# One exponential over both heads' scores in an attention and feed-forward kernel

## The reference

```python
x = x + xattn(layernorm(x), ctx, mask, g_norm, null_kv, Wq, Wkv, Wout, g_out)
x = x + ffn(layernorm(x), k0, k1, k2, s0, s1, s2)
```

## Time and profile before

| | us |
|---|---|
| median of three runs | 1582.44 |
| span of the profiled execution | 1574.0 |
| time around the span (median less span) | 8.4 |
| TensorE matmul busy | 1513.6 |
| VectorE busy | 1032.6 |
| GpSimd busy | 777.9 |
| ScalarE busy | 708.4 |
| of that the exponentials of line 777, 832 of them | 527.5 |
| attention steps, first to last score matmul | 130.3 to 1326.3 |

### The profile page before, as it was taken

One profiled execution on the slowest core, in us unless ns is written; L12 is line 12 of the kernel. 1 busy time (PEld: TensorE's weight loads), 2 busy tenths in 40 slices (PEclk: granted clock), 3 DMA queues, 4 the chain that ended last, 5 costly groups with the idle time before them and its releaser, 6 DMA issues.

```text
span 1574.0 us, 20245 instructions
## 1 busy us (share of the span) xinstructions
PE 1513.6 (96%) x6068; PEld 845.3 (54%) x6068; DVE 1032.6 (66%) x1272; ACT 708.4 (45%) x1169; POOL 777.9 (49%) x657
## 2 busy tenths in 40 slices
PE   5898999999999999999999999999999998999998
PEld 3554555455545544554455445554554453778777
DVE  7784677577767766776677567757776747544442
ACT  3324444644464446445544554455445534232242
POOL 3005666576656665666566566656665646101100
PEclk9998999999999999999999999999999999999999
DMA  5222100110020002000200020003000501101000
GB/s 160 79 82 68 51 7 7 34 57 8 12 60 26 7 16 77 7 8 14 77 7 8 15 77 7 11 10 84 8 8 21 178 7 61 61 14 53 13 14 14
DMA packets 43586, 60.22 MB, mean 38 GB/s; under 512 B 4049, under 2 KB 31636, under 8 KB 42580
## 3 DMA queue, kind: packets, MB, share of 16 engines
q1 hardware_dynamic: 43476, 58.92, 12.7%
HBM read 26.27 MB, written 17.30 MB: 28 GB/s over the span
## 4 chain that ended last, share of the span: by engine, by line
PE 89%; DVE 5%; issue 2%; ACT 2%; POOL 1%; DMA 0%; DVEq 0%; SPq 0%; ACTq 0%; POOLq 0%
PE ps_o L1244 25%; PE ps_s L1263 17%; PE ps_s L1264 12%; PE ps_side L1182 12%; PE ps_side L1325 10%; PE ps_side L1168 3%; PE ps_s L1286 3%; PE ps_side L1203 2%; PE ps_side L1158 1%; PE ps_side L1159 1%; DVE mxh L925 1%; PE ps_side L1191 1%; PE ps_o L1142 1%; PE ps_o L1144 1%; DVE khl L914 1%
## 5 line engine op out<-in xcount | busy, mean ns | idle before, releaser
L424 POOL TENSOR_TENSOR acc<-acc,prob 128x512 f32<-128x512 f32 x522 | 669.1, 1299 | 338.5 <-ACT prob L777 311.9
L777 ACT ACTIVATE prob<-ps_s,keybias 128x512 f32<-128x512 f32 x832 | 527.5, 685 | 560.7 <-PE ps_s L1264 518.4
L925 DVE TENSOR_REDUCE mxh<-ps_side 128x1 f32<-128x804 f32 x512 | 485.6, 991 | 152.9 <-PE ps_side L1182 150.3
L1244 PE MATMUL ps_o<-prob,vp 128*64 128x512 f32 x1664 | 448.2, 616 | 0.0
L1263 PE MATMUL ps_s<-qdup,khl 128*128 128x512 f32 x832 | 373.0, 448 | 9.2 <-issue 4.6
L1263 PEld LDWEIGHTS ps_s<-qdup,khl 128*128 128x128 f32 x832 | 156.1, 188 | 365.5 <-issue 261.9
L1264 PE MATMUL ps_s<-qrest,krest 128*128 128x512 f32 x832 | 329.5, 396 | 0.0
L1182 PE MATMUL ps_side<-khl,qdup 128*128 128x402 f32 x1024 | 249.3, 360 | 10.5 <-ACTq L716 4.2
L1182 PEld LDWEIGHTS ps_side<-khl,qdup 128*128 128x128 f32 x1024 | 187.3, 189 | 58.5 <-DVE mxh L925 22.3
L424 DVE TENSOR_TENSOR acc<-acc,prob 128x512 f32<-128x512 f32 x182 | 166.8, 918 | 60.5 <-ACT prob L777 50.2
L1264 PEld LDWEIGHTS ps_s<-qrest,krest 128*128 128x128 f32 x832 | 157.3, 189 | 19.0 <-issue 0.4
(11 more groups left out here) (130 smaller groups left out, 1039.3 us busy)
## 6 DMA issues: line engine op xcount, KB each, us to landing
o_scratch<-onorm SPq DMA_DIRECT2D x32, 256.0 KB, 2.1
otb<-o_scratch SPq DMA_DIRECT2D x4, 2048.0 KB, 8.1
qdup<-qdup SPq DMA_DIRECT2D x14, 512.0 KB, 5.3
v_scratch<-vsb SPq DMA_DIRECT2D x13, 512.0 KB, 3.2
krest<-khl SPq DMA_DIRECT2D x16, 416.0 KB, 5.1
vp<-v_scratch SPq DMA_DIRECT2D x8, 832.0 KB, 7.4
xs<-in_x SPq DMA_DIRECT2D x4, 512.0 KB, 6.8
xres<-in_x SPq DMA_DIRECT2D x1, 2048.0 KB, 11.1
```

Of the source, the lines that this page charges most:

```text
L424: eng.tensor_tensor(a, so_far, prob[g][s % RING][:, :], ALU.add).then_inc(sum_done[g], 1)
L777: act.activation(prob[g][s % RING][:, :], ps_s[g][:, :], ACT.Exp, bias=keybias[:, kt:kt + 1], scale=SCALE).then_inc(p_made[g], 1)
L925: dve.reduce_max(mxh[:, g, qt, half:half + 1], ps_side[slot][:, :, 0:MXW], AX.XY).then_inc(side_free[slot], 1)
L1244: last = pe.matmul(ps_o[qb % 2][hi_rows(g), :], vp[u][:, kt, hi_rows(g)], prob[g][s % RING][:, :], start=(kt == 0), stop=(kt == KT - 1))
```

## The change

The two PSUM tiles of the scores become one tile of two banks, and `ps_s[g]` are its halves. The two rings `prob[g]` become one ring whose tiles hold both heads, and `prob[g][r]` are their halves. ScalarE waits for both heads' scores and both heads' sums and for `pv_done`, and then issues one exponential over 2 x 512 columns. The two semaphores `p_made[g]` become one, which this exponential raises by one. All waits for `p_made[g]` (in `add_tile`, in `values` and ahead of each head's scores) become waits for it. The matmuls, the sums, the side jobs and their order are the same.

```diff
--- before.py
+++ after.py
@@ -256,7 +256,8 @@
         cT1 = sb("cT1", [C1, KPAD])
         at["vp0"] = at[""]
         vp = [sb(f"vp{u}", [P, KT, P]) for u in range(2)]
-        prob = [[sb(f"prob{g}{r}", [P, QW]) for r in range(RING)] for g in range(2)]
+        prob_both = [sb(f"prob{r}", [P, 2, QW]) for r in range(RING)]
+        prob = [[prob_both[r][:, g, :] for r in range(RING)] for g in range(2)]
         acc = [[sb(f"acc{g}{r}", [P, QW]) for r in range(2)] for g in range(2)]
         x_lo = sb("x_lo", [P, DC, SEQ], F32R)
         onorm = sb("onorm", [P, QW])
@@ -318,7 +319,8 @@
         assert at["small"] <= end_operands0, (at["small"], end_operands0)
 
 
-        ps_s = [psum(f"ps_s{g}", [P, 512]) for g in range(2)]
+        ps_both = psum("ps_s", [P, 2, 512])
+        ps_s = [ps_both[:, g, :] for g in range(2)]
         ps_o = [psum(f"ps_o{r}", [P, 512]) for r in range(2)]
         ps_side = [psum(f"ps_side{r}", [P, 2, 512]) for r in range(2)]
         ps_c = ps_s
@@ -353,7 +355,7 @@
         mx_made, row_made = sem("mx_made"), [sem("row_made0"), sem("row_made1")]
         s_made = [sem(f"s_made{g}") for g in range(2)]
 
-        p_made = [sem(f"p_made{g}") for g in range(2)]
+        p_made = sem("p_made")
         pv_done = sem("pv_done")
         sum_done = [sem(f"sum_done{g}") for g in range(2)]
         o_copied = sem("o_copied")
@@ -418,7 +420,7 @@
 
             qb, kt = s // KT, s % KT
             a = acc[g][qb % 2][:, :]
-            eng.wait_ge(p_made[g], 1 + STEPS * n + s + 1)
+            eng.wait_ge(p_made, 1 + STEPS * n + s + 1)
             eng.wait_ge(sum_done[g], CREDIT + (KT - 1) * (QB * n + qb) + kt - 1)
             so_far = prob[g][(s - 1) % RING][:, :] if kt == 1 else a
             eng.tensor_tensor(a, so_far, prob[g][s % RING][:, :], ALU.add).then_inc(sum_done[g], 1)
@@ -671,8 +673,7 @@
 
         @block.scalar
         def _(act):
-            act.sem_inc(p_made[0], 1)
-            act.sem_inc(p_made[1], 1)
+            act.sem_inc(p_made, 1)
             act.sem_inc(f_free, 3)
 
             def wait_side(j, pair):
@@ -772,10 +773,10 @@
                     freed = consumed(s - RING) + CREDIT if s >= RING else consumed(STEPS + s - RING) + CREDIT - (KT - 1) * QB
                     for g in range(2):
                         act.wait_ge(s_made[g], STEPS * n + s + 1)
-                        act.wait_ge(pv_done, STEPS * n + s + 1)
                         act.wait_ge(sum_done[g], (KT - 1) * QB * n + freed)
-                        act.activation(prob[g][s % RING][:, :], ps_s[g][:, :], ACT.Exp,
-                                       bias=keybias[:, kt:kt + 1], scale=SCALE).then_inc(p_made[g], 1)
+                    act.wait_ge(pv_done, STEPS * n + s + 1)
+                    act.activation(prob_both[s % RING][:, :, :], ps_both[:, :, :], ACT.Exp,
+                                   bias=keybias[:, kt:kt + 1], scale=SCALE).then_inc(p_made, 1)
                     for j, job in plan[s]:
                         side(j, job, pair)
                 if last:
@@ -1240,7 +1241,7 @@
                 if kt == 0:
                     pe.wait_ge(norm_done, 4 * n + qb + 1)
                 for g in range(2):
-                    pe.wait_ge(p_made[g], 1 + STEPS * n + s + 1)
+                    pe.wait_ge(p_made, 1 + STEPS * n + s + 1)
                     last = pe.matmul(ps_o[qb % 2][hi_rows(g), :], vp[u][:, kt, hi_rows(g)], prob[g][s % RING][:, :],
                                      start=(kt == 0), stop=(kt == KT - 1))
                 last.then_inc(pv_done, 1)
@@ -1259,7 +1260,7 @@
                     qb, kt = s // KT, s % KT
                     qs, ks = slice(qb * QW, (qb + 1) * QW), slice(kt * P, (kt + 1) * P)
                     for g in range(2):
-                        pe.wait_ge(p_made[g], 1 + STEPS * n + s)
+                        pe.wait_ge(p_made, 1 + STEPS * n + s)
                         pe.matmul(ps_s[g][:, :], khl[u][g][:, ks], qdup[u][g][:, qs], start=True, stop=False)
                         pe.matmul(ps_s[g][:, :], krest[u][g][:, ks], qrest[u][g][:, qs], start=False,
                                   stop=True).then_inc(s_made[g], 1)
```

## The result

The changed kernel takes 1616.63 us (median of 4 runs, 1615.27 to 1617.78), where the kernel before had 1582.26 in runs beside it. The ratio is 1.0223, with a 95% interval from 1.0207 to 1.0238: slower by 34 us. The profiled execution took 1615.27 us with a span of 1613.2. The forecast was 1617.

A forecast was written before the change was run, and what follows sets the result against it. TensorE, busy 96%, was taken to bound the kernel. Terms 19.4 + 1.6 + 2.7 + 12.2 - 1.1 = 34.8 us gave span 1608.8 and, with 8.4, median 1617 us; range 1607 to 1634, own range 1610 to 1625, chance 0.76.

The forecast's parts named there:

- The exponential's length: ScalarE's double-width exponential: 1.11 us, from 0.832 ns a column in the PSUM copies, between bounds of 685 and 1270 ns.
- the rival's 1635: Joining saves nothing: the exponential over two banks takes 1.27 us, 116 steps pay 0.16 more, 1635 us; chance 0.11.
- Start and release: Bare step: 0.80 to the second matmul, delay 0.51 (last pair 0.43), exponential 1.11, release 0.055; 2.48 or 2.40 us.
- the 6 us that I had allowed for it: Handling of waits in the paying steps: bounds of 0.05 us a step either way, 6 us; taken as zero.
- Bare steps, first seven pairs: Eight bare steps in each of seven pairs: 56 steps go from 2.13 to 2.48 us, 19.4 us in all.
- Step 49: Step with a small MX job on TensorE: period 2.25 us before, 7 x 0.23 = 1.6 us more.
- Step 31: Step with MX and SA: TensorE's wait for ScalarE's copy, 0.60 us, grows by 0.38; 7 x 0.38 = 2.7 us.
- Last pair: 46 bare steps go from 2.13 to 2.40 us, 12.2 us more; 1.1 given back in steps 34 to 46.
- Nothing elsewhere: SA and L steps stay at 2.87 and 3.00 us, VectorE and GpSimd equally busy, end span unchanged: no cost.
- most is given back: Longer steps shrink waits for VectorE and GpSimd: at the most about 10 us come back, 1607 us; chance 0.06.
- The clock did not fall: Rival: holes in 46 bare steps of the last pair bring TensorE the lower clock, about 1700 us; chance 0.03.
- the 8.4 us: Amount by which the median lies above the profiled span, added to the span of 1608.8 to give 1617.

The follow-up runs named there:

- late-start kernel: The kernel before, with head 0's exponential waiting for head 1's scores too and each bank still released by itself: 1590.77 us, ratio 1.0069.

## Why the prediction was right

The mechanism and the time were right: 1617 forecast, 1616.6 measured. On the profile 34.8 us were forecast and 39.2 found. Not all terms were right.

- *The exponential's length.* 1.111 us from the slope of the copies; measured 1.116. The kernel with two exponentials behind joint waits shows that at 1.27 the time would have been 1635.4, which is the rival's 1635.
- *Start and release.* The 0.80 and the 0.055 were right (0.81 and 0.05). The delay between the last scores and the exponential was the mis-sized term: I kept 0.51 for the loop pairs and 0.43 for the last one, with zero for a change in the handling of waits. It is 0.47 in the loop pairs and 0.56 in the last and the first. The step that failed is "Two further waits stand behind the one for the scores, then as now". Neither half holds: before, none stood behind it in the unrolled pairs and one in the loop pairs; after, three and one. The error is inside the 6 us that I had allowed for it.
- *Bare steps, first seven pairs.* 19.4 forecast for 56; measured 45 x 0.32 + 0.41 + 8 x 0.39 = 17.9 for 54. In the two others the loop turns round, and what they paid can't be told from that. I had also counted the first pair as a loop pair, though it is unrolled.
- *Step 49.* 1.6 forecast; 6 x 0.19 and 0.27 in the first pair, 1.4 measured.
- *Step 31.* 2.7 forecast, 6 x 0.44 + 0.46 = 3.1 measured. TensorE's second SA job waits 1.05 us where it waited 0.60:

```profile
537.73 0.25 ACT L714 ACTIVATE rowbuf<-ps_side 16x128 fp32r<-16x128 f32 x1
...
538.08 0.63 PE L1183 MATMUL ps_side<-khl,qdup 128*128 128x402 f32 x2 [1.05 <-ACTq L717]
```

- *Last pair.* 12.2 - 1.1 = 11.1 forecast, 15.3 measured. Its bare steps pay 0.39 each and not 0.27, which makes 17.6 for the 45 ahead of step 51. Of that 2.3 are given back and not 1.1, in the steps where TensorE waited before behind VectorE and GpSimd. Steps 41 and 44 went from 4.93 and 3.92 to 3.60 and 2.53, but the waits for sums moved more than they went: 39, 43 and 45 grew from 2.13 to 2.88, 3.40 and 3.22. The direction was right, and the two errors (5.4 too few paid, 1.2 too few given back) partly cancel.
- *Nothing elsewhere.* Right for the first seven pairs: SA and L steps are equal to 0.01 us, though the sums grow, on GpSimd from 727.3 to 738.9 us and those of the form acc<-acc,prob on VectorE from 166.8 to 173.3. The prediction had both engines' busy time unchanged. The layout is not the reason: with it alone the sums on GpSimd take 728.2. In the last pair sums are on the path, as the rows below show, and what their growth costs there was not separated. Head 0's sums were said to start 0.95 us later; the prediction's own numbers give 0.9.

```profile
1332.23 1.11 ACT L778 ACTIVATE prob<-ps_s,keybias 128x1024 f32<-128x1024 f32 x1 [1.77 <-DVE acc L426]
...
1333.40 0.50 PE L1264 MATMUL ps_s<-qdup,khl 128*128 128x512 f32 x1 [0.68 <-ACT prob L778]
```

- *The rivals.* That most is given back is wrong: 2.3 of 10 us. The clock did not fall in the last pair: its window has a granted clock of 1.00 (the third number from the right).

```profile
1217.50:1364.00 146.50, 129.99 (x489) 58.12 (x490) 73.65 (x84) 56.85 (x51) 80.47 (x55) 1.00 0.22 71
```

The spans differ by 4.4 us more than the forecast, of which the last pair has 4.2. Between the medians the difference is 34.4 us, and 36.7 or 35.9 beside the later medians of before. So that the median was met to 0.4 us owes something to luck: the span of before lay at the low end of its runs, and I took the 8.4 us around it for a constant, while every later profile has 2 us between span and time.

## What to carry to other kernels

Joining two instructions halves their count, and it also joins their start conditions and their releases. Where two buffers in alternation are all that decouples two engines, the joined one makes them take turns. Work out the loop (last producer's end, delay, instruction, release) and hold it against the other work that the waiting engine has in each kind of step: here a saving on an engine that is 45% busy and off the path was worth nothing, and the steps without cover paid the whole difference. Cover put in by moving other work must be checked against that work's own reader.

## What was not expected of the hardware

*Waits that are met already.* Each one handled behind the last to be met delays the exponential by some 0.04 us: 0.43 us from the last score matmul's start with none behind, 0.47 to 0.48 with one, 0.52 with two, 0.56 with three. Their order is not that of the source. The count is not the whole of it: in the loop pairs of before a register instruction carries the wait for the scores, one further wait stands behind, and the delay is 0.51. In the late-start kernel such an instruction stands behind as one of two, and the delay is 0.56.

*The loop boundary.* In every profile TensorE waits 1.9 to 4.5 us between pairs 3 and 4 and between 5 and 6, where the loop of two pairs turns round; the profile calls it issue. Afterwards the clock sometimes falls. Before, and then after, at the start of the fourth pair:

```profile
587.29 0.49 PE L1263 MATMUL ps_s<-qdup,khl 128*128 128x512 f32 x1 [2.09 <-issue]
587.62 0.40 PE L1264 MATMUL ps_s<-qrest,krest 128*128 128x512 f32 x1
587.85 0.39 PE L1263 MATMUL ps_s<-qdup,khl 128*128 128x512 f32 x1
```

```profile
596.72 0.65 PE L1264 MATMUL ps_s<-qdup,khl 128*128 128x512 f32 x1 [1.89 <-issue]
597.16 0.63 PE L1265 MATMUL ps_s<-qrest,krest 128*128 128x512 f32 x1
597.59 0.63 PE L1264 MATMUL ps_s<-qdup,khl 128*128 128x512 f32 x1
```

The granted clock of the changed kernel in this stretch (the third number from the right):

```profile
596.00:600.00 4.00, 3.28 (x7) 2.21 (x8) 0.00 (x0) 1.11 (x1) 0.95 (x1) 0.61 0.05 14
```

In the first the matmuls start 0.33 and 0.23 us apart. In the second they start 0.44 and 0.43 apart, the granted clock is 0.61 over 596 to 600, a mean of the clock's two levels (1.2 and 2.4 GHz), and the step takes 5.15 us in place of 3.53. The wait was the shorter one, 1.89 against 2.09. Before it TensorE had been through bare steps with holes in them, but the holes are not needed: the kernel with only the layout changed has none, and it has this slow step twice in its profile, with waits of 1.92 and 3.75 us. The kernel before has waits of 2.09 and 2.53 and no slow step. The two turns of the loop with the steps behind them cost 4.8 us in the profile of before, 9.0 in that of the layout kernel and some 13 in that of the late start, which is the 8 us of that kernel's profile. Executions of before differ by up to 9 us, and the granted clock goes with that in the 36 that stand beside the experiments: it was 0.994 to 0.995 in the four shortest (1575.40 to 1576.87 us) and 0.989 to 0.991 in the three longest (1583.69 to 1584.06). Whether these falls come at the loop's turns too, and what makes the cost of a turn vary, was not tried.
